# Scatter-add of expert results on one Trainium2 core: forty tiles in groups of four, first and second choices as separate adds

## What is computed

```python
scores = jax.nn.sigmoid(x @ gate_w)
_, selected = jax.lax.top_k(scores + expert_bias[None, :], 2)      # first and second choice of 16 experts
top_scores = jnp.take_along_axis(scores, selected, axis=1)
top_scores = top_scores / (top_scores.sum(-1, keepdims=True) + 1e-20)
comb = jnp.zeros((T, 16)).at[jnp.arange(T)[:, None], selected].add(top_scores)
for e in range(16):
    g, u = jnp.split(x @ experts_gate_up[e], 2, axis=-1)
    routed = routed + comb[:, e:e + 1] * (jax.nn.silu(g) * u @ experts_down[e])
return shared + routed
```

## Time and profile before

| | us |
|---|---|
| median of 3 runs | 1226.7 (1224.17 to 1230.62) |
| the profiled execution, its own time | 1228.2 |
| its span in the trace | 1226.3 |
| first `y` copy of the tile loop starts | 947.62 |
| first add is issued | 949.30 |
| last add is issued | 1219.45 |

### The profile page before, as it was taken

The page is one execution under the profiler, slowest core; times in us unless marked ns, Lnnn a source line. Parts: engine busy times, 40 slices in busy tenths (PEclk is TensorE's granted clock), DMA queues, the critical chain, the costliest instruction groups (busy, mean ns, idle before and its releaser), DMA issues. The chain is left out here.

```text
span 1226.3 us, 31125 instructions
## 1 busy us (share of the span) xinstructions
PE 1171.7 (96%) x13185; PEld 579.9 (47%) x13186; DVE 692.5 (56%) x1146; ACT 475.2 (39%) x669; POOL 316.1 (26%) x457
## 2 busy tenths in 40 slices
PE   6999999999999999999999999999999999999996
PEld 3444434444445544445546554544444444444442
DVE  3743596756787665668675786878566222221220
ACT  3321323533555453555453455555522222222221
POOL 6012311221321320221122131111102434344443
PEclk9999999999999999999999999999999999999999
DMA  8320775104294201364500245100146665667540
GB/s 196 104 85 24 203 152 118 29 15 118 72 157 84 73 24 30 86 119 103 114 11 15 101 87 87 72 3 3 71 148 202 140 151 136 178 187 231 150 91 14
DMA packets 113057, 122.17 MB, mean 100 GB/s; under 512 B 18928, under 2 KB 78448, under 8 KB 112800
## 3 DMA queue, kind: packets, MB, share of 16 engines
q1 hardware_dynamic: 101968, 99.11, 31.6%
q0 software_dynamic: 10528, 21.12, 8.5%
q10 hardware_dynamic: 432, 0.08, 0.0%
HBM read 94.63 MB, written 28.97 MB: 101 GB/s over the span
## 5 line engine op out<-in xcount | busy, mean ns | idle before, releaser
L681 DVE TENSOR_REDUCE mx<-ps_m 128x2 f32<-128x1024 f32 x256 | 312.9, 1222 | 194.9 <-PE ps_m L1018 189.5
L888 ACT ACTIVATE prob<-ps_s 128x1024 f32<-128x1024 f32 x256 | 261.9, 1023 | 322.8 <-PE ps_s L1018 322.0
L1018 PE MATMUL acc<-xnT,wring 128*32 128x512 f32 x1888 | 248.5, 593 | 0.6 <-DVE first_z L617 0.6
L1833 PE MATMUL ps_gu<-ring,xgT 128*128 x376 | 176.9, 593 | 2.1 <-issue 1.1
L1018 PE MATMUL ps_s<-q_stack,k_stack 99*32 99x512 bf16 x2048 | 161.5, 380 | 4.4 <-ACT prob L888 3.8
L1018 PE MATMUL ps_m<-k_stack,q_stack 96*32 96x512 bf16 x1952 | 153.0, 380 | 9.5 <-DVE mx L681 7.9
L1543 DVE COPY xgT<-ps_x 128x512 f32<-128x512 f32 x47 | 32.5, 692 | 207.4 <-PE ps_x L1805 198.4
L1203 PE MATMUL ps_o<-prob,values 128*32 128x128 f32 x4096 | 138.4, 273 | 0.0
L1203 PEld LDWEIGHTS ps_o<-prob,values 128*32 128x32 f32 x4096 | 116.2, 110 | 44.8 <-issue 39.3
L1018 PEld LDWEIGHTS ps_m<-k_stack,q_stack 96*32 96x32 bf16 x1952 | 55.1, 96 | 127.8 <-issue 72.7
L1501 POOL DMA_INDIRECT out<-y,dest x47 | 74.4, 1584 | 154.1 <-DMA out<-y,dest 117.6
(11 more groups left out here) (282 smaller groups left out, 1178.0 us busy)
## 6 DMA issues: line engine op xcount, KB each, us to landing
ring<-in_w_experts SPq DMA_DIRECT2D x96, 256.0 KB
wring<-in_w_in SPq DMA_DIRECT2D x80, 256.0 KB, 3.8
q_stack<-part_rows SPq DMA_DIRECT2D x96, 128.0 KB, 4.9
wring<-in_w_out SPq DMA_DIRECT2D x32, 256.0 KB, 2.8
part_rows<-part SPq DMA_DIRECT2D x20, 384.0 KB, 4.9
xt<-in_x SPq DMA_DIRECT2D x16, 256.0 KB, 4.3
out<-x SPq DMA_DIRECT2D x4, 1024.0 KB, 4.8
k_stack<-part_rows SPq DMA_DIRECT2D x48, 64.0 KB, 3.0
```

The lines of the kernel that those rows point to most:

```text
L681: nc.vector.tensor_reduce(mx[:, n % G, 2 * u:2 * u + 2], ps_m[:, :, :], AX.X, ALU.max).then_inc(s_max, 1)
L888: nc.scalar.activation(prob[:, slot % PROB, :, :], ps_s[:, :, :], ACT.Exp, scale=SCALE).then_inc(s_exp, 1)
L1018: ins = nc.tensor.matmul(dst[c:c + 32, :], stationary[:, c:c + 32], moving, start=start, stop=stop, tile_position=(0, c))
L1833: ins = nc.tensor.matmul(ps_gu[p][:, :], xgT[:, p, k * P:(k + 1) * P], weights(own)[:, k * 2 * F:(k + 1) * 2 * F], start=(k == 0), stop=(k ...
```

## The change

The token's name now carries a sign: `place` is multiplied by -1 for second choices, so `listed` is positive for a first choice, negative for a second, zero for an empty slot. DVE makes three tables of destinations where it made one: side 0 with all rows, side 1 with first choices only, side 2 with second choices only; a row that isn't on a side gets the number past the end. No token has two first choices, so adds of side 1 touch different rows from each other, and so do adds of side 2.

Tiles 0 to 39 go in ten groups (`WAVE` = 4). In a group POOL issues for each tile its side 1 add and the gather of tile n+6, then waits until the four side 1 adds have landed, issues the four side 2 adds, and at the start of the next group waits until these have landed. Tiles 40 to 46 go as before, one add for all rows, each after the one before it has landed. `YB` becomes 8, and ACT waits for the whole group of the tile eight places back.

```diff
-    YB = 4
+    WAVE = 4
+    WAVED = 10 * WAVE
+    YB = 2 * WAVE
...
-            for n in range(TILES):
+            def add_rows(n, rows, done):
+                pool.indirect_dma_start(
+                    out=out[:, :], out_offset=bass.IndirectOffsetOnAxis(ap=dest[:, rows, n:n + 1], axis=0),
+                    in_=y[:, n % YB, :], in_offset=None, bounds_check=TOKENS - 1, oob_is_err=False,
+                    compute_op=ALU.add).then_inc(done, 16)
+
+            for w in range(0, WAVED, WAVE):
+                if w:
+                    pool.wait_ge(s["second_added"], 16 * w)
+                for n in range(w, w + WAVE):
+                    pool.wait_ge(s["yc"], n + 1)
+                    add_rows(n, 1, s["first_added"])
+                    pool.wait_ge(s["share"], n + 1)
+                    load_x(n + XG)
+                pool.wait_ge(s["first_added"], 16 * (w + WAVE))
+                for n in range(w, w + WAVE):
+                    add_rows(n, 2, s["second_added"])
+            pool.wait_ge(s["second_added"], 16 * WAVED)
+            for n in range(WAVED, TILES):
                 pool.wait_ge(s["yc"], n + 1)
-                if n:
-                    pool.wait_ge(s["added"], 16 * n)
-                pool.indirect_dma_start(
-                    out=out[:, :], out_offset=bass.IndirectOffsetOnAxis(ap=dest[:, n:n + 1], axis=0),
-                    in_=y[:, n % YB, :], in_offset=None, bounds_check=TOKENS - 1, oob_is_err=False,
-                    compute_op=ALU.add).then_inc(s["added"], 16)
+                if n > WAVED:
+                    pool.wait_ge(s["added"], 16 * (n - WAVED))
+                add_rows(n, 0, s["added"])
                 if n + XG < TILES:
                     pool.wait_ge(s["share"], n + 1)
                     load_x(n + XG)
...
-                nc.vector.tensor_scalar(place[:, i, :], iota_h[:, :], lo[:, k, t:t + 1], None, ALU.is_equal
-                                        ).then_inc(s["place"], 1)
+                nc.vector.tensor_scalar(place[:, i, :], iota_h[:, :], lo[:, k, t:t + 1], -1.0 if k else 1.0,
+                                        ALU.is_equal, ALU.mult).then_inc(s["place"], 1)
             dve.wait_ge(s["inverse"], 1)
-            nc.vector.tensor_scalar(token[:, :], ps_h[0][:, 0:TILES], -1.0, 0.0, ALU.add, ALU.max).then_inc(s["token"], 1)
             V.then(nc.vector.tensor_copy(listed[:, :], ps_h[0][:, 0:TILES]))
+            V.then(nc.vector.scalar_tensor_tensor(out=sides[:, 0, :], in0=listed[:, :], scalar=-1.0, in1=listed[:, :],
+                                                  op0=ALU.mult, op1=ALU.max))
+            nc.vector.tensor_scalar(token[:, :], sides[:, 0, :], -1.0, 0.0, ALU.add, ALU.max).then_inc(s["token"], 1)
...
-            V.then(nc.vector.tensor_scalar(empty[:, :], listed[:, :], 0.0, beyond[:, 0:1], ALU.is_equal, ALU.mult))
-            nc.vector.scalar_tensor_tensor(out=dest[:, :], in0=listed[:, :], scalar=-1.0, in1=empty[:, :],
+            nc.vector.tensor_scalar(sides[:, 1, :], listed[:, :], 0.0, None, ALU.max)
+            V.then(nc.vector.tensor_scalar(sides[:, 2, :], listed[:, :], -1.0, 0.0, ALU.mult, ALU.max))
+            V.then(nc.vector.tensor_scalar(empty[:, :, :], sides[:, :, :], 0.0, beyond[:, 0:1], ALU.is_equal, ALU.mult))
+            nc.vector.scalar_tensor_tensor(out=dest[:, :, :], in0=sides[:, :, :], scalar=-1.0, in1=empty[:, :, :],
                                            op0=ALU.add, op1=ALU.add).then_inc(s["dest"], 1)
...
                 if n >= YB:
-                    act.wait_ge(s["added"], 16 * (n - YB + 1))
+                    if n - YB < WAVED:
+                        act.wait_ge(s["second_added"], 16 * WAVE * ((n - YB) // WAVE + 1))
+                    else:
+                        act.wait_ge(s["added"], 16 * (n - YB - WAVED + 1))
```

More of the change, by code:

```diff
@@ L1370, in experts_phase @@
         listed = sb("listed", [P, TILES])
-        empty = sb("empty", [P, TILES])
+        empty = sb("empty", [P, 1 + TOP, TILES])
         beyond = sb("beyond", [P, 1])
         token = sb("token", [P, TILES], mybir.dt.uint32)
-        dest = sb("dest", [P, TILES], mybir.dt.uint32)
+        dest = sb("dest", [P, 1 + TOP, TILES], mybir.dt.uint32)
+        sides = sb("sides", [P, 1 + TOP, TILES])
         mask = sb("mask", [P, TILES, E])
@@ L1411, in experts_phase @@
                  "sd", "sacc", *(f"xg{i}" for i in range(XG)), "tx", "txc", "gu", "sg", "h", "th", "thc", "dn", "yc",
-                 "gates", "gst", "x1st", "late", "share", "dest", "mask", "added", "v", "ones")
+                 "gates", "gst", "x1st", "late", "share", "dest", "mask", "first_added", "second_added", "added", "v", "ones")
         s = {n: sem("e_" + n) for n in signals}
@@ L1463, in _ @@
             ready(E - 1)
-            sp.wait_ge(s["added"], 16 * TILES)
+            sp.wait_ge(s["first_added"], 16 * WAVED)
+            sp.wait_ge(s["second_added"], 16 * WAVED)
+            sp.wait_ge(s["added"], 16 * (TILES - WAVED))
         @block.gpsimd
```

## The result

| | before | after |
|---|---|---|
| median of 3 runs | 1226.7 us | 1258.4 us (1256.95 to 1259.5) |
| profiled execution, span | 1226.3 us | 1257.6 us |
| ratio, 95% interval | | 1.0235 (1.0198 to 1.0272) |

The change makes the kernel 2.3% slower, 32 us. The forecast was 1250 us, 1.9%.

The account below looks back on a forecast made before the run. PE (5.81 us a tile) and POOL's add chain ran nearly neck and neck; grouped, POOL would set the pace. Group 1 at 983.2, plus 226.8 and 9 for weights, gave 1219.0; plus 30.9 and 0.4, 1250 us; 8-in-10 range 1236 to 1268.

Parts of the forecast that it names:

- The main step: POOL's adds: rows per add halve, adds double, issue stays 1.55 us with no row against 1.59 for a full add.
- The fixed part of a group: POOL's issues and gaps for 8 adds and 4 gathers, without the two landings: 18.39 us.
- loop's start against before: DVE ahead of the loop: one more instruction and `token` third instead of first, 0.3 us, from 0 to 0.6.
- first `y` to the add of tile 4: Group 0 at PE's pace, then landings of 3.8 and 3.5 us; group 1 starts at 983.2.
- nine groups: POOL's groups 1 to 9 at 25.2 us each, 226.8 us, with 9 us more for the weights.
- add of tile 40 to the end: Single adds as before: 24.04 us to the last issue and 6.85 to the span's end, 30.9 us.
- the weights' share: Weight transfers lengthening landings: 25 us before, scaled by POOL's landing waits from 73% to 27%, 9 us.
- rival 1: Half-empty adds land nearly as fast as empty ones, 2.0 us; a group 22.4 us, kernel 1221 us; 4%.
- rival 2: An add's issue gets shorter with fewer rows, say 0.8 us; a group 18.9 us, kernel 1221 us; 2%.
- Rival 3: A group's adds queue behind one another and the gathers; landings 4.2 us, weights 14 us, kernel 1270 us; 14%.
- Rival 4: Landings of 2.8 us and half the weights' share; a group 24.0 us, kernel 1235 us; 14%.
- My price for keeping PE's pace: If POOL keeps up, PE's gaps and the lag at the end go: 1226.7 - 6.1 + 0.3 = 1221 us.

Follow-up runs that it names:

- the half-filled chain: Against the kernel with the new tables but the old one-add-per-tile loop: each add takes side 1 only, second choices left out; 1225.3 us, ratio 0.9975.
- the run with cut transfers: Changed kernel with weight transfers of experts 4 to 15 cut to 16 columns per piece; 1239.8 us, ratio 1.0076.
- the run with empty adds: Changed kernel with every destination past the end, so no routed row is added, issues and waits as they are; 1227.4 us, ratio 0.998.
- gathers in the waits: Changed kernel with a group's four gathers moved, two into each landing wait; 1227.5 us, ratio 0.9999; run again 1226.2 us, ratio 0.9985.
- first choices only: Changed kernel without the side 2 adds of tiles 0 to 39, a group waiting for side 1 adds alone; 1225.2 us, ratio 0.9978.
- the experiment with the tables alone: Changed kernel with the old loop, one add per tile with all rows; new tables and eight result buffers stay; 1232.5 us, ratio 1.0031.
- the one with 79: Against the kernel with gathers moved into the landing waits: groups for tiles 0 to 31 only, single adds behind them; 1229.6 us, ratio 1.0006 of before.

## Why the prediction was right, and where it was off

**The main step held.** "The change halves the rows of each add but doubles the number of adds, and the issue doesn't get shorter with fewer rows": 1.56 us on average over 87 adds. The fixed part of a group was forecast at 18.39 us and is 18.3. Quiet landings were near what was taken: in the group shown, whose last tile has 37 first and 40 second choices, 3.3 us was taken and 3.49 and 3.31 came; in the last group (61 and 67) 3.7 was taken and 3.48 and 3.49 came; the half-filled chain has 3.72 for 55 rows. A quiet group was forecast at 25.2 on average, and the one shown takes 25.1. That the eight buffers let PE and ACT keep their distance, that POOL never waits for a `y` in the middle, and that PE starves for gathered rows held too. Two signs came out otherwise in their shape. The groups were to be 25 to 27 us apart; their mean is 26.7, and single ones take from 24.0 to 31.0. And PE's waits come as seven of up to 6.5 us instead of one of 2 to 3 us in every group.

**Term by term**, against the forecast span of 1249.9 (measured 1257.6):

| term | forecast | measured |
|---|---|---|
| loop's start against before | +0.3 | +4.2, of it 3.05 before the changed phase |
| first `y` to the add of tile 4 | 35.3 | 36.9 (the side 2 landing 5.5 for 3.5) |
| nine groups | 226.8 + 9 (weights) | 240.0 |
| add of tile 40 to the end | 30.9 | 28.9 |

The mis-sized term is the weights' share. I had scaled the excess of landings before by the share of the time in which POOL waits for one (73% down to 27%) and got 9 us; the run with cut transfers puts it at 16 to 19 us: 14 to 17 in the nine groups and 2 in group 0, for which I had put nothing. Over the nine groups the error is partly hidden by landings that I had taken too long: without weights they come to 223.2 us, 24.8 a group, where I had 226.8. The tail gave back another 2.0 us. That the sum comes within 8 us of the span is thus in part luck. The 25 us that I scaled down was itself low: I had taken 4.2 us for every quiet full tile before, and the trace has many at 3.8 to 4.1. Why the share is so much larger isn't shown. The rows of the adds aren't needed for it, since landings of 5.6 to 6.5 us are there with every row dropped. A transfer can delay any of the four adds of a half and with it the end of the half, not just what's in flight while POOL waits; that is argued, not tested.

The start was under-priced too: 1.1 us in this profile, up to 2.9 in others, where I had taken 0.3 and held 0.6 for the most. Up to the first gather it is 0.45 us (29.65 from the phase's start, 29.20 before), within what I had held; the rest is a longer issue of the first gather and, in three kernels, a lower clock, both told in the last section.

**The rivals.** Empty-like landings (rival 1) would have brought 1221: the run with empty adds shows the mechanism is right (22.2 us for a quiet group, under PE's 23.24), and its condition isn't met, since a half-filled add lands in 3.3 to 3.7 us and not 2. By the fit of the Trainium skill (DMA: Bandwidth & Descriptors, "Anatomy of one DMA — SWDGE (gpsimd) path") it would land in 2.3 us, an estimate from its figures. Here the fixed part agrees (1.93 to 2.0 us with no rows, counted from the end of the issue) and the slope doesn't (3.72 us for 55 rows, 4.20 for 128). Shorter issues (rival 2) fall by the 1.55 us of an add with no row at all. Rival 3, landings of 4.2 from queueing, falls: 3.49 us right behind a gather. Its time, 1270, was 12 us too high where the forecast was 8 too low, and its 14 us for the weights was nearer to what they cost than the forecast's 9. Rival 4, 2.8 us and half the weights, falls on both counts: quiet landings are 3.25 us on average (24.8 less 18.3, halved), and the weights cost more, not less. My price for keeping PE's pace (1221) was too low by 4 to 6 us: the three kernels in which the slowdown is gone (empty adds, gathers in the waits, first choices only) take 1225 to 1227.5, beside a kernel before of 1228 to 1229 in those runs. The longer start and the lag at the end are in there.

## What to carry to other kernels

An indirect DMA has a price per instruction on the engine that issues it, here 1.55 us with no rows and 1.59 with 128: splitting one in two to gain freedom of order pays twice the issue. Before splitting, add up the issuing engine's time per period, issues plus every landing that it waits out, and compare it with the period of the engine that sets the pace; a wait of 3.5 us that looked free is the place to put the issues that depend on nothing, as the gathers here. And look at what the last landing of the chain is worth at all: here the most that could be gained was 0.5%.

## What wasn't expected of the hardware

**PE's clock fell after a wait of some microseconds.** Timeline of PE in the changed kernel, around its longest wait (start, duration, idle before):

```profile
1107.53 1.11 PE L1833 MATMUL ps_x<-ident,xg 128*128 128x128 f32 x4 [6.54 <-DMA xg<-xn_rows,token]
1108.43 3.62 PE L1877 MATMUL acc<-ring,hT 128*128 x4
...
1116.54 1.88 PE L1877 MATMUL acc<-ring,hT 128*128 x4
```

Four matmuls of the same line take 3.62 us right after the wait and 1.88 eight us later. The granted clock is 0.50 from 1107.5 to 1112.0 and 1.00 from 1116.5 to 1120.0, the levels of 1.2 and 2.4 GHz. The changed kernel has seven such waits: after those of 4.68, 5.10 and 6.54 us the transposition that follows takes 1.11 or 1.12 us, after those of 0.34 to 3.17 us it takes 0.66. By stretches (us, PE busy, granted clock, DMA share, GB/s), the one with the wait of 4.68 us, which ends at 1050.62, and the next without a wait:

```profile
1041.00:1055.00 14.00, 9.32 (x22) 0.76 0.57 129
1055.00:1069.00 14.00, 14.00 (x45) 1.00 0.71 182
```

So a starved PE pays for the wait and then for the slow matmuls behind it. Here it was hidden, since POOL set the pace. It isn't hidden at the loop's start: the first gate-up (eight matmuls) took 3.70 us in most kernels here and 5.39 in three of those with the new tables:

```profile
939.60 5.39 PE L1861 MATMUL ps_gu<-ring,xgT 128*128 x8 [0.98 <-DVE xgT L1564]
```

(the kernel with few weights). The granted clock is 0.68 over those 5.4 us and 1.00 over the same matmuls of the changed kernel. Why it fell in three kernels and not in the others isn't shown: in the 4.6 us before, PE was busy for 2.77 us in this kernel and for 2.81 in the changed one. The slow gate-up is 1.7 of the 2.9 us by which the start is longer in the experiment with the tables alone. The other 1.1 or 1.2 us are in all kernels with the new tables: 0.45 before the first gather, 0.62 in its issue, which is 1.87 us long in them and 1.25 in the kernel before, for a reason that I can't name.

**The end of the span** comes 6.8 us after the last add's issue begins in kernels with 47 adds, 5.7 in the one with 79 and 4.5 in those with 87. The 2.3 us between first and last, less 0.35 us that the last seven adds lose, are the 2.0 us which the tail gave back, and it isn't explained.
